# Last stage of a four-layer block: round two's opening and round one's closing moved beside other work

## Chip, cores and metric

One Trainium2 chip, one core. The metric is device time in microseconds (us) of one launch. The kernel before takes 3154.64 us, the median of three runs (3143.95 to 3157.51 us).

## What is computed

The program runs four residual layers over x of shape (4, 1024, 128): a state-space layer, a mixture of experts with top-2 routing, an attention with two softmaxes and their difference, and last a layer of soft experts. The change touches the last one alone, so it is the one shown (`_layernorm` around it and within it, `_gating` for both of its halves):

```python
n1 = _layernorm(x, ln1_w, ln1_b)                       # x is itself a layernorm of the residual
rw = _gating(n1, smha_sim, smha_gates, 2)              # normalize, 8 logits, top 2, softmax
q = einsum('btc,ech,bte->bth', n1, q_proj, rw)         # and k, v: 8 experts each
attn = softmax(mask(q @ k.T * scale)) @ v              # causal, t = 1024
hs = x + einsum('bth,ehc,bte->btc', attn, o_proj, rw)
n2 = _layernorm(hs, ln2_w, ln2_b)
rw2 = _gating(n2, moe_sim, moe_gates, 2)
inter = gelu(einsum('btc,eci->btei', n2, w1))
return hs + einsum('btei,eic,bte->btc', inter, w2, rw2)
```

The result is normalized once more and added to the residual x, and that is the output.

## The kernel before

The stage works on the four batches in two rounds, r = 0 and r = 1. In each, batches k = 0 and k = 1 of the round run side by side: everything is written once per k, with its own half of PSUM (four banks, B[0] to B[3]) and its own SBUF tiles. In a round, per k:

- **Opening**: statistics and normalization of x into hs (`stats`, `norms`: DVE L256, L260, L265; the square root is `rstd` on POOL, L248 and L250), the same again into n1, weight and bias (DVE L1318, L1323), squares of n1 (POOL L1469), transposes of n1 (PE L1591) copied to xT (ACT L1518), eight logits per row (PE L1603), and the gate: normalize, top 2, softmax (DVE L1330 to L1370, POOL L1472, ACT L1522). It ends in the weights rw.
- **Projections**, 16 steps q (two halves of 512 rows by 8 experts). POOL multiplies n1 by one expert's weight (L1486), PE transposes the result into B[3] (`scaled`, L1614), ACT takes its high half (L1537), DVE its low half (L1392), and PE makes the products (L645 to L647 for q and k, L1665 for v). PE transposes step q + 1 just ahead of the products of q. A multiply of q waits for the transpose of q - 2, since s_sc has two buffers.
- **Attention**, 8 rows of blocks i: scores (PE L1625), mask and maximum (DVE L1406, L1408), exponential (ACT L1552), transposes (PE L1685) and copies (ACT L1560), the product with v (PE L1695), its scaling (DVE L1398), the reciprocal (DVE L1414).
- **Output**: 16 more multiplies, transposes (PE L1709), copies and products (PE L1723).
- **Second opening** for n2, with the same helpers, then the **experts** (PE L1738 and L1751, ACT L1579, DVE L1438, POOL add L1495).
- **Closing**: statistics and normalization of hs into lnb, and the addition to X (POOL L1502); SP stores it.

What sets the order: each engine has one instruction queue, in order. For each engine there are two generators (`soft_dve(e, 0)`, `soft_dve(e, 1)` and so on), one per k, that yield planned times; `weave` always takes the generator with the smallest time. The planned times decide only the order of the instructions in a queue; the waits on semaphores decide when each runs. The plan is in `D_LN`, `D_TR`, `D_GATE`, `D_ATT`, `d_scaled`, `d_proj`; round two has the same plan `D_PERIOD = 193` later:

```python
def weave(*streams):
    ...
    while live:
        s = min(live)
        t = next(s[2], None)
```

Since a generator goes through a round and then through the next, all of round two of one k stands behind all of its round one in every queue.

Of the kernel before, what the change touches and what calls it, by code (L numbers as in the profile page):

```python
# [104 lines left out]
def program(nc, d, out):  # L105
    ctx = ExitStack()
    with ctx:
# [1085 lines left out]
        def d_at(k, r, t):  # L1193
            return D_PERIOD * r + D_SHIFT * k + t

        def d_scaled(k, r, q, more=0.0):

            if q >= 16:
                return d_at(k, r, D_OUT + D_STEP * (q - 16) - 1.5 + more)
            h, x = q // 8, q % 8  # L1200
            return d_at(k, r, 24 + 26.2 * h if x == 0 else 25 + 26.2 * h + D_EXPERT * (x - 1))

        def d_proj(k, r, q, more=0.0):
            return d_at(k, r, 25 + 26.2 * (q // 8) + D_EXPERT * (q % 8) + more)
# [4 lines left out]
        def two(name, *ordered):  # L1209

            return [Tick(sem(f"{name}{k}"), [(r, *x) for r in range(2) for x in ordered]) for k in range(2)]

        t_dtr = two("t_dtr", (0, 0), (0, 1), (0, "logits"), (2, 0), (2, 1), (2, "logits"))
# [5 lines left out]
        a_dtr = two("a_dtr", (0, 0), (0, 1), (0, "exp"), (2, 0), (2, 1), (2, "exp"))  # L1219
# [3 lines left out]
        v_dln = two("v_dln", *keys(4, ("stats", "out")))  # L1223
        v_dgt = two("v_dgt", *keys((0, 2), ("sumsq", "logits", "pre", "rw")))
# [3 lines left out]
        p_dln = two("p_dln", *[x for w in range(4) for x in [(w, "rstd")] + ([(2 * w - 2, "sq"), (2 * w - 2, "norm")]  # L1228
                                                                              if w in (1, 2) else [])])
# [10 lines left out]
        s_hs, s_n1, s_q, s_k, s_v = [[MA[:, 5120 * k + 1024 * i:5120 * k + 1024 * i + 1024] for k in range(2)]  # L1240
                                     for i in range(5)]
        s_hs, s_n1, s_v = [[x.rearrange("p (j c) -> p j c", c=128) for x in y] for y in (s_hs, s_n1, s_v)]
# [4 lines left out]
        s_g = [big[7][:, 512 * k:512 * k + 512].rearrange("p (j n) -> p j n", j=8) for k in range(2)]  # L1247
# [55 lines left out]

        def soft_dve(e, k):
            s, L = st[f"d{k}"], s_L[k]
            hs, n1 = s_hs[k], s_n1[k]
            hst, n1t = [hs[:, j, :] for j in range(8)], [n1[:, j, :] for j in range(8)]
            B, S0, S1 = bank[4 * k:4 * k + 4], ps[2 * k], ps[2 * k + 1]

            def G(i):  # L1310
                return s_g[k][:, :, 8 * i:8 * i + 8]

            def affine(r, w):
                norms(e, s, hst, n1).then_inc(*dve_own.up())
                ready = dve_own.now()
                yield d_at(k, r, D_LN[w][1] + 1)
                e.wait_ge(*ready)
                e.tensor_tensor(n1, n1, lnp[:, 2 * w - 2:2 * w - 1, :].to_broadcast([128, 8, 128]), ALU.mult).then_inc(  # L1318
                    *dve_own.up())
                ready = dve_own.now()  # L1320
                yield d_at(k, r, D_LN[w][1] + 2)
                e.wait_ge(*ready)
                e.tensor_tensor(n1, n1, lnp[:, 2 * w - 1:2 * w, :].to_broadcast([128, 8, 128]), ALU.add).then_inc(  # L1323
                    *v_dln[k].up(r, w, "out"))

            def gating(r, w, times):
                which = w // 2
                yield d_at(k, r, times[1])
# [548 lines left out]
```

## Time and profile before

| what | value |
|---|---|
| median of three runs | 3154.64 us (3143.95 to 3157.51) |
| the profiled execution, its own time | 3154.66 us |
| its span, first to last instruction | 3152.5 us |
| mean granted TensorE clock | 0.869 |
| busy: PE, DVE, ACT, POOL | 2425.7, 2198.9, 1710.0, 1415.3 us |
| the last stage | from 2505.4 us to the end |
| round one of it: projections | 2553.7 to 2636.2 us |
| round one: attention, output | 2636.2 to 2689.1, 2689.1 to 2731.9 us |
| round one: experts on PE | 2751.8 to 2818.0 us |
| round two: first transpose of the projections | 2869.6 us |

The page gives busy times by engine over the whole span, the span in 40 slices, the chain that ended last and the costliest groups. Busy shares over the whole program say little here, since four layers with different limits stand one behind the other; the stage is read from the timeline and from tables of stretches. The granted clock is 1.00 at full speed (2.4 GHz) and 0.50 at half of it (1.2 GHz).

### The profile page before, as it was taken

What the parts mean: (1) busy time and instruction counts of PE and PEld (TensorE: products, weight loads), DVE (VectorE), ACT (ScalarE), POOL (GpSimd) and SP (SyncE); (2) the same over time, 40 slices, a digit from 0 to 9 for tenths busy, and PEclk for the clock granted to TensorE, in tenths of its full rate; (3) what the DMA queues carried; (4) which work ended last, traced back from release to release, by engine and by line L of the source; (5) the groups of instructions that cost most, each with busy time, mean ns of one, the idle gap of its engine ahead of it and who ended that gap; (6) DMA issues with size and microseconds to landing.
All of it is one profiled execution on the core that took longest, in us unless ns stands there. A gap on an engine that the chain in (4) does not pass through costs nothing.

```text
span 3152.5 us, 42236 instructions
## 1 busy us (share of the span) xinstructions
PE 2425.7 (77%) x15570; PEld 1750.1 (56%) x15570; DVE 2198.9 (70%) x3701; ACT 1710.0 (54%) x2608; POOL 1415.3 (45%) x1331
## 2 busy tenths in 40 slices
PE   3114776677667687799999999999999569876987
PEld 1002455344345565477777777777777456755675
DVE  3995698699699612588878887887888543355334
ACT  4223664666376242588777877787778323222332
POOL 0341144144224300365765676657656641564156
PEclk8556888788788888799999999999999879887988
DMA  3000000000000000100000010010000100000000
GB/s 100 0 0 0 0 1 1 1 1 1 1 1 1 1 1 14 41 21 21 21 21 21 21 28 21 20 26 21 21 24 9 41 1 1 1 14 1 1 1 14
DMA packets 32029, 42.02 MB, mean 13 GB/s; under 512 B 8897, under 2 KB 18130, under 8 KB 31442
## 3 DMA queue, kind: packets, MB, share of 16 engines
q1 hardware_dynamic: 31826, 39.34, 4.6%
q8 instruction: 125, 2.05, 0.3%
q14 instruction: 78, 0.64, 0.1%
HBM read 12.05 MB, written 2.10 MB: 4 GB/s over the span
## 4 chain that ended last, share of the span: by engine, by line
PE 46%; issue 19%; DVE 17%; POOL 12%; ACT 4%; SPq 1%; DMA 0%; POOLq 0%; ACTq 0%; DVEq 0%
PE ps L954 10%; PE ps L932 6%; PE ps L943 6%; POOL MA L379 5%; DVE MA L1090 3%; PE ps L710 3%; PE ps L914 2%; PE ps L1723 2%; DVE lnb L265 2%; PE ps L645 2%; PE ps L647 1%; PE ps L646 1%; PE ps L1665 1%; POOL MA L1173 1%; PE ps L1625 1%
## 5 line engine op out<-in xcount | busy, mean ns | idle before, releaser
L1090 DVE TENSOR_REDUCE MA<-ps 128x1 f32<-128x1024 f32 x512 | 623.3, 1221 | 195.3 <-PE ps L932 182.7
L379 POOL TENSOR_TENSOR MA<-MA,BIG 128x1024 f32<-128x1024 f32 x120 | 280.2, 2356 | 624.9 <-DVE BIG L350 624.9
L954 PE MATMUL ps<-MA,WB 128*64 128x128 f32 x4096 | 502.5, 276 | 0.0
L954 PEld LDWEIGHTS ps<-MA,WB 128*64 128x64 f32 x4096 | 440.7, 137 | 88.4 <-issue 87.4
L344 DVE TENSOR_TENSOR_SCAN BIG<-BIG 128x1024 f32<-128x1024 f32 x128 | 347.1, 2751 | 0.0
L932 PE MATMUL ps<-BIG 96*128 96x512 f16 x1024 | 314.6, 389 | 13.5 <-ACT WB L1017 5.1
L632 ACT ACTIVATE HR<-ps,b 128x512 f32<-128x512 f32 x288 | 191.6, 687 | 243.9 <-PE ps L647 242.9
L710 PEld LDWEIGHTS ps<-WB,HR 128*128 128x128 f32 x2304 | 307.3, 210 | 24.9 <-issue 8.6
L710 PE MATMUL ps<-WB,HR 128*128 128x128 f32 x2304 | 314.4, 295 | 0.0
L1017 ACT ACTIVATE WB<-ps,MA 128x1024 f32<-128x1024 f32 x206 | 229.6, 1115 | 149.8 <-DVE MA L1090 149.8
L497 PE MATMUL ps<-bc,sel 96*128 96x512 bf16 x256 | 108.3, 520 | 247.1 <-DVE BIG L350 190.8
L1024 ACT ACTIVATE MA<-ps 128x1024 f32<-128x1024 f32 x256 | 259.9, 1015 | 6.0 <-PE ps L943 6.0
L1486 POOL TENSOR_TENSOR BIG<-MA,BIG 128x512 f32<-128x512 f32 x128 | 132.1, 1049 | 232.3 <-PE ps L1709 74.5
L436 ACT ACTIVATE BIG<-MA,aneg 128x1024 f32<-128x1024 f32 x128 | 141.5, 1142 | 109.9 <-DVE BIG L344 105.8
L1017 ACT ACTIVATE MA<-ps,MA 128x1024 f32<-128x1024 f32 x153 | 170.7, 1116 | 45.7 <-DVE MA L1090 45.6
L1147 POOL TENSOR_TENSOR MA<-MA 128x2 f32<-128x2 f32 x128 | 25.2, 197 | 369.5 <-DVE MA L1094 369.5
L497 PEld LDWEIGHTS ps<-bc,sel 96*128 96x128 bf16 x256 | 22.3, 113 | 300.1 <-DVE BIG L350 213.1
L943 PE MATMUL ps<-ident,WB 128*128 128x128 f32 x1232 | 165.9, 278 | 5.9 <-POOL WB L1159 3.1
L943 PEld LDWEIGHTS ps<-ident,WB 128*128 128x128 f32 x1232 | 144.4, 144 | 45.1 <-DVE WB L1099 10.6
L645 PE MATMUL ps<-xT,WB 128*128 128x512 f16 x288 | 126.4, 439 | 52.9 <-ACT HR L632 48.7
L589 DVE SCALAR_TENSOR_TENSOR acc<-ps,g,acc 128x128 f32<-128x128 f32 x256 | 71.1, 338 | 123.1 <-PE ps L710 123.1
L340 DVE TENSOR_TENSOR BIG<-MA,ps 128x1024 f32<-128x1024 f32 x128 | 149.8, 1210 | 1.2 <-PE ps L497 1.2
(290 smaller groups left out, 5166.3 us busy)
## 6 DMA issues: line engine op xcount, KB each, us to landing
BIG<-BIG SPq DMA_DIRECT2D x192, 64.0 KB, 2.0
BIG<-WB SPq DMA_DIRECT2D x192, 64.0 KB, 2.0
WB<-w_dram SPq DMA_DIRECT2D x1, 2304.0 KB, 14.7
X<-x_dram SPq DMA_DIRECT2D x4, 512.0 KB, 12.6
HR<-w_dram SPq DMA_DIRECT2D x1, 2048.0 KB, 9.4
out_dram<-X SPq DMA_DIRECT2D x4, 512.0 KB, 3.2
WB<-wqkv_dram SPq DMA_DIRECT2D x1, 1536.0 KB, 6.7
WB<-w_dram SPq DMA_DIRECT2D x2, 512.0 KB, 9.1
```

The costliest lines, as they stand in the source:

```text
L340: e.tensor_tensor(db[k][c], du[:, c, :], ps[0][:, :], ALU.mult).then_inc(*v_mtb.up(b, n, c))
L344: e.tensor_tensor_scan(db[k][c], da[k][c], db[k][c], 0.0, ALU.mult, ALU.add).then_inc(*v_mscan.up(b, n, c))
L379: e.tensor_tensor(yy[:, c, :], yy[:, c, :], db[n % 2][c], ALU.add).then_inc(*p_my.up(b, n, c))
L632: e.activation(hr[(4 * k + f) % 8], bank[4 + f % 2], ACT.Gelu, bias=small["b1"][:, PLAN[k][1], f:f + 1], scale=BACK).then_inc(*a_fg.up(b, ...
L645: e.matmul(o, w[0], x[0], start=first, stop=False)
L710: i = e.matmul(o, hr[(4 * kk + f) % 8][:, 128 * j:128 * j + 128], w2[:, x, f, :], start=f == 0 and x != 8, stop=f == 3)
L932: x = e.matmul(ps[s][:, 512 * h:512 * h + 512], stack[q % 2][0:96, 0, 2 * pp + s, 128 * i:128 * i + 128], stack[q % 2][0:96, 1, 2 * pp + s ...
L943: x = e.transpose(ps[2][:, 128 * k:128 * k + 128], P_of(n, 0)[:, 128 * k:128 * k + 128], ident[:, :])
L954: x = e.matmul(bank[6][64 * pp:64 * pp + 64, 0:128], V[(4 * b + g) % 2][:, k, 64 * pp:64 * pp + 64], DT[n % 2][:, 128 * k:128 * k + 128], ...
L1017: e.activation(P_of(n, s), ps[s][:, :], ACT.Exp, bias=L[:, 2 * s + pp:2 * s + pp + 1], scale=1.0, accum_out=L[:, 4 + 2 * s + pp:5 + 2 * s ...
L1024: e.activation(DT[n % 2], ps[2][:, :], ACT.Copy, scale=1.0).then_inc(*a_at.up(n))
L1090: e.tensor_reduce(L_of(n)[:, c:c + 1], ps[s][:, :], AX, ALU.max, negate=True).then_inc(*v_amx.up(n, s))
```

## The change

Round two's opening gets generators of its own (`front_pe`, `front_act`, `front_dve`, `front_pool`, one for each r and k), and so does each round's closing (`last_dve`, `last_pool`). With their own planned times (`F_LN`, `F_TR`, `F_LOGITS`, `F_GATE`, `D_LN[1]`) their instructions stand among those of the other generators: round two's normalizations among round one's projections (planned 32 to 55), its transposes and logits between the projections and the scores (75.2, 77.6), its gate in round one's attention (78.2 to 88); round one's closing (191.5 and 195.5) among round two's projections, since `D_PERIOD` goes from 193 to 164. Buffers: hs, n1 and the gate's tile exist once per round (n1 of round two in what was `sel`, its gate tile in `acc`), the experts' products go to `s_tmp` instead of `s_sc`. Round two's transposes and logits use bank B[3] for both halves, so the second transpose waits for ACT's copy of the first, and the first product with v waits until DVE has read the logits. In the gate, the part from the subtraction on has a planned time of its own behind both k's first part. No arithmetic is added or left out.

```diff
-        D_PERIOD, D_EXPERT, D_SHIFT = 193.0, 3.15, 0.0
-        D_LN = [(0, 3), (5, 8), (139.5, 142.5), (187.5, 190.5)]
-        D_TR = [11, 110, 145.5]
-        D_GATE = [(13, 16, 19, 22), (145.5, 148.5, 151.5, 154.5)]
+        D_PERIOD, D_EXPERT = 164.0, 3.15
+        D_LN, D_TR, D_LOGITS, D_GATE = [(139.5, 142.5), (191.5, 195.5)], 145.5, 151.5, (145.5, 148.5, 151.5, 152, 154.5)
+        F_LN = [[(0, 3), (5, 8)], [(32, 36), (40, 44)]]
+        F_TR, F_LOGITS, F_GATE = [11, 75.2], [18.9, 77.6], [(13, 16, 19, 19.5, 22), (49, 55, 78.2, 82, 88)]
...
+        def front_dve(e, k, r):
+            s, hs = st[f"d{k}"], s_hs[k][r]
+            xs, hst = [tile_of(k + 2 * r, j) for j in range(8)], [hs[:, j, :] for j in range(8)]
+            yield F_LN[r][0][0]
+            stats(e, s, xs, {}).then_inc(*v_dln[k].up(r, 0, "stats"))
+            yield F_LN[r][0][1]
+            e.wait_ge(*p_dln[k].at(r, 0, "rstd"))
+            norms(e, s, xs, hs).then_inc(*v_dln[k].up(r, 0, "out"))
+            yield F_LN[r][1][0]
+            stats(e, s, hst, {0: v_dln[k].at(r, 0, "out")}).then_inc(*v_dln[k].up(r, 1, "stats"))
+            yield F_LN[r][1][1]
+            e.wait_ge(*p_dln[k].at(r, 1, "rstd"))
+            yield from d_affine(e, k, r, 1, F_LN[r][1])
+            yield from d_gate(e, k, r, 0, F_GATE[r], bank[4 * k + (3 if r else 2)])
...
+        def last_dve(e, k, r):
+            s, hst = st[f"d{k}"], [s_hs[k][r][:, j, :] for j in range(8)]
+            yield d_at(r, D_LN[1][0])
+            stats(e, s, hst, {0: p_dm[k].at(r, 15)}).then_inc(*v_dln[k].up(r, 3, "stats"))
+            yield d_at(r, D_LN[1][1])
+            e.wait_ge(*p_dln[k].at(r, 3, "rstd"))
+            if r:
+                e.wait_ge(*p_dx[k].at(r - 1))
+            norms(e, s, hst, lnb[k]).then_inc(*v_dln[k].up(r, 3, "out"))
...
+        def front_pool(e, k, r):
+            for w in range(2):
+                yield F_LN[r][w][0]
+                d_root(e, k, r, w)
+            yield from d_norm(e, k, r, 0, F_GATE[r])
...
+                for q in range(32):
+                    h, x = q // 8 % 2, q % 8
+                    yield d_scaled(r, q, -4 if r and q < 2 else 0)
...
+                    if q >= 2:
+                        e.wait_ge(*t_dst[k].at(r, q - 2))
+                    elif r:
+                        e.wait_ge(*t_dst[k].at(r - 1, 30 + q))
...
+        def last_pool(e, k, r):
+            yield d_at(r, D_LN[1][0])
+            d_root(e, k, r, 3)
+            yield d_at(r, D_LN[1][1])
+            e.wait_ge(*v_dln[k].at(r, 3, "out"))
...
+        def front_act(e, k, r):
+            B = bank[4 * k:4 * k + 4]
+            yield F_TR[r]
+            d_turned(e, k, r, 0, (B[3], B[3]) if r else B)
+            yield F_GATE[r][3] + 2
+            d_exp(e, k, r, 0)
...
+        def d_turn(e, k, r, w, banks):
+            for h in range(2):
+                e.wait_ge(*v_dln[k].at(r, max(w, 1), "out"))
+                if w == 0 and r:
+                    if h:
+                        e.wait_ge(*a_dtr[k].at(1, 0, 0))
...
+        def front_pe(e, k, r):
+            B = bank[4 * k:4 * k + 4]
+            yield F_TR[r]
+            d_turn(e, k, r, 0, (B[3], B[3]) if r else B)
+            yield F_LOGITS[r]
+            d_logits(e, k, r, 0, B[3 if r else 2])
...
                     else:
                         e.wait_ge(*v_dlo[k].at(r, 15))
+                        if r == 0:
+                            e.wait_ge(*v_dgt[k].at(1, 0, "logits"))
```

How the queues change, at three places. **POOL, round one's projections.** Before, all 64 multiplies of the projections and of the output (L1486) stand in a row:

```order
L1472 TENSOR_TENSOR BIG<-BIG,half 128x8 x2
L1486 TENSOR_TENSOR BIG<-MA,BIG 128x512 x64
L248 TENSOR_SCALAR st_d<-st_d 128x8
```

Now (the multiply is L1502, the squares are L1477):

```order
L1502 TENSOR_TENSOR BIG<-MA,BIG 128x512 x8
L248 TENSOR_SCALAR st_d<-st_d 128x8
L250 TENSOR_TENSOR st_d<-st_d,half 128x8
L248 TENSOR_SCALAR st_d<-st_d 128x8
L250 TENSOR_TENSOR st_d<-st_d,half 128x8
L1502 TENSOR_TENSOR BIG<-MA,BIG 128x512 x4
L248 TENSOR_SCALAR st_d<-st_d 128x8
L250 TENSOR_TENSOR st_d<-st_d,half 128x8
L248 TENSOR_SCALAR st_d<-st_d 128x8
L250 TENSOR_TENSOR st_d<-st_d,half 128x8
L1502 TENSOR_TENSOR BIG<-MA,BIG 128x512 x4
L1477 TENSOR_TENSOR BIG<-sel 128x1024 x2
```

Two pairs of square roots and one pair of squares now stand between the multiplies of steps 3 and 4, 5 and 6, 7 and 8.

**POOL, from round one's experts to round two's projections.** Now (L1514 is the experts' addition, L1502 the multiply of round two, L1523 the addition to X):

```order
L1514 TENSOR_TENSOR MA<-MA,BIG 128x512 x31
L1502 TENSOR_TENSOR BIG<-sel,acc 128x512 x2
L1514 TENSOR_TENSOR MA<-MA,BIG 128x512
L1502 TENSOR_TENSOR BIG<-sel,acc 128x512 x2
L248 TENSOR_SCALAR st_d<-st_d 128x8
L250 TENSOR_TENSOR st_d<-st_d,half 128x8
L248 TENSOR_SCALAR st_d<-st_d 128x8
L250 TENSOR_TENSOR st_d<-st_d,half 128x8
L1502 TENSOR_TENSOR BIG<-sel,acc 128x512 x4
L1523 TENSOR_TENSOR X<-X,lnb 128x1024 x2
L1502 TENSOR_TENSOR BIG<-sel,acc 128x512 x56
```

The closing's roots stand behind the multiplies of steps 0 and 1, its additions to X behind those of steps 2 and 3.

**DVE, round one's attention**, row of blocks 1 to row 2. Before (L1414 reciprocal, L1406 mask, L1408 maximum):

```order
L1414 RECIPROCAL BIG<-BIG 128x1 x2
L1406 TENSOR_TENSOR ps<-ps,tri 128x128
L1408 TENSOR_REDUCE BIG<-ps 128x1
```

Now the first rows of what stands behind the reciprocals (L1431 is the reciprocal; L1349 to L538 are subtraction and top 2 of one k):

```order
L1431 RECIPROCAL BIG<-BIG 128x1 x2
L1349 TENSOR_TENSOR acc<-acc,sgm 128x8x8
L527 MAX acc<-acc 128x8 x8
L531 MAX_INDEX gi<-acc 128x8 x8
L534 CAST acc<-gi 128x8x8
L537 TENSOR_TENSOR acc<-iota,acc 128x8x8
L538 TENSOR_TENSOR acc<-iota,acc 128x8x8
L1349 TENSOR_TENSOR acc<-acc,sgm 128x8x8
```

All of the gate from the subtraction to the exponential, for both k, stands between the reciprocals of row 1 and the mask of row 2.

## Rows read from the trace of the kernel before

**Rows 1.** The page: the head.
```profile
span 3152.5 us, 42236 instructions
```
**Rows 2.** Busy times by stretch: stretch, its length, busy (instructions) of PE, PEld, DVE, ACT, POOL, PEclk, DMA.
```profile
2553.70:2636.20 82.50, 80.20 (x705) 56.19 (x705) 22.05 (x33) 23.61 (x41) 32.20 (x31) 0.96 0.00 1
2636.20:2689.10 52.90, 43.38 (x267) 32.34 (x265) 22.13 (x63) 25.57 (x60) 4.11 (x4) 1.00 0.00 1
2818.00:2869.60 51.60, 10.33 (x50) 10.23 (x49) 46.01 (x237) 4.19 (x7) 28.38 (x22) 0.54 0.07 21
```
**Rows 3.** Timeline, one step of the projections: start, length, instruction, [idle before, releaser].
```profile
2603.41 0.60 PE L1614 MATMUL ps<-ident,BIG 128*128 128x128 f32 x4
2608.21 0.60 PE L1614 MATMUL ps<-ident,BIG 128*128 128x128 f32 x4
...
2605.76 0.69 DVE L1392 SCALAR_TENSOR_TENSOR BIG<-ps,BIG 128x512 f16<-128x512 f32 x1 [0.39 <-ACT BIG L1537]
...
2604.09 2.13 POOL L1486 TENSOR_TENSOR BIG<-MA,BIG 128x512 f32<-128x512 f32 x2 [2.68 <-PE ps L1614]
```
**Rows 4.** Timeline from round one's last expert products to round two's first products.
```profile
2814.28 3.73 PE L1751 MATMUL ps<-WB,HR 128*128 128x128 f32 x32
...
2816.14 4.93 POOL L1495 TENSOR_TENSOR MA<-MA,BIG 128x512 f32<-128x512 f32 x4 [1.02 <-DVE BIG L1438]
...
2873.08 0.63 PE L645 MATMUL ps<-BIG,WB 128*128 128x512 f16 x1
```
**Rows 5.** Timeline, round two's first statistics and square roots.
```profile
2830.69 1.63 DVE L256 BATCH_NORM_STATS2 st_d<-X 128x6 f32<-128x128 f32 x8
...
2835.71 1.71 POOL L250 TENSOR_TENSOR st_d<-st_d,half 128x8 f32<-128x8 f32 x1
```
**Rows 6.** Timeline, round two's normalization into n1, weight, bias and squares.
```profile
2843.95 4.39 DVE L265 TENSOR_SCALAR MA<-MA,st_d 128x128 f32<-128x128 f32 x16
...
2851.83 4.66 POOL L1469 TENSOR_TENSOR BIG<-MA 128x1024 f32<-128x1024 f32 x2 [5.66 <-DVE MA L1323]
```
**Rows 7.** Timeline, round two's closing.
```profile
3139.62 6.43 DVE L265 TENSOR_SCALAR lnb<-MA,st_d 128x128 f32<-128x128 f32 x16
...
3141.84 2.34 POOL L1502 TENSOR_TENSOR X<-X,lnb 128x1024 f32<-128x1024 f32 x1
```
**Rows 8.** Timeline, the start of round one's attention.
```profile
2634.40 0.60 ACT L1542 ACTIVATE MA<-ps 128x512 f32<-128x512 f32 x1 [4.63 <-PE ps L647]
...
2636.19 0.44 PE L1625 MATMUL ps<-MA 128*128 128x128 f32 x2
2638.81 0.92 PE L1625 MATMUL ps<-MA 128*128 128x128 f32 x4 [2.18 <-ACT MA L1543]
...
2640.51 0.70 PE L1625 MATMUL ps<-MA 128*128 128x256 f32 x2 [0.66 <-ACT WB L1552]
...
2643.30 0.28 DVE L1406 TENSOR_TENSOR ps<-ps,tri 128x128 f32<-128x128 f32 x1
```
**Rows 9.** Logits of both k; then DVE's busy time in the gate's three parts.
```profile
2747.89 4.07 PE L1603 MATMUL ps<-simn,xT 128*128 128x8 f32 x32
...
2545.43:2548.10 2.67, 2.53 (x29) 0.50 0.00 0
2549.23:2551.53 2.30, 2.16 (x18) 0.50 0.00 0
```
**Rows 10.** PE busy and granted clock around three pauses of PE.
```profile
509.90:515.20 5.30, 0.01 (x1) 1.00 0.00 0
515.20:518.50 3.30, 3.26 (x8) 0.50 0.00 0
...
533.47:539.10 5.63, 5.29 (x23) 0.50 0.00 0
...
2744.78:2747.51 2.73, 2.73 (x13) 0.50 0.00 0
2747.51:2750.90 3.39, 3.39 (x33) 1.00 0.02 5
```

More of the change, by code:

```diff
@@ L1222, in program @@
         a_dg = two("a_dg", *keys(16))
-        v_dln = two("v_dln", *keys(4, ("stats", "out")))
-        v_dgt = two("v_dgt", *keys((0, 2), ("sumsq", "logits", "pre", "rw")))
+        v_dln = two("v_dln", *keys((2, 3), ("stats", "out")), front=keys(2, ("stats", "out")))
+        v_dgt = two("v_dgt", *keys((2,), ("sumsq", "logits", "pre", "rw")), front=keys((0,), ("sumsq", "logits", "pre", "rw")))
         v_dlo, v_dat = two("v_dlo", *keys(16)), two("v_dat", *[x for i in range(9) for x in
@@ L1302, in experts_pe, with d_affine @@
             e.matmul(bank[0][:, 0:16], ones[:, :], lsq[:, 0:16], start=True, stop=True).then_inc(*t_dsp.up(0))
+        def d_affine(e, k, r, w, times):
+            s, hs, n1 = st[f"d{k}"], s_hs[k][r], s_n1[k][r]
+            norms(e, s, [hs[:, j, :] for j in range(8)], n1).then_inc(*dve_own.up())
+            ready = dve_own.now()
+            yield times[1] + 1
+            e.wait_ge(*ready)
+            e.tensor_tensor(n1, n1, lnp[:, 2 * w - 2:2 * w - 1, :].to_broadcast([128, 8, 128]), ALU.mult).then_inc(
+                *dve_own.up())
+            ready = dve_own.now()
+            yield times[1] + 2
+            e.wait_ge(*ready)
+            e.tensor_tensor(n1, n1, lnp[:, 2 * w - 1:2 * w, :].to_broadcast([128, 8, 128]), ALU.add).then_inc(
+                *v_dln[k].up(r, w, "out"))
@@ L1304, in soft_dve @@
         def soft_dve(e, k):
             s, L = st[f"d{k}"], s_L[k]
-            hs, n1 = s_hs[k], s_n1[k]
-            hst, n1t = [hs[:, j, :] for j in range(8)], [n1[:, j, :] for j in range(8)]
-            B, S0, S1 = bank[4 * k:4 * k + 4], ps[2 * k], ps[2 * k + 1]
+            B, S0 = bank[4 * k:4 * k + 4], ps[2 * k]
             def G(i):
[L1311 to L1324, printed above, removed]
@@ new lines, in d_turn @@
+        def d_turn(e, k, r, w, banks):
+            for h in range(2):
+                e.wait_ge(*v_dln[k].at(r, max(w, 1), "out"))
+                if w == 0 and r:
+                    if h:
+                        e.wait_ge(*a_dtr[k].at(1, 0, 0))
+                    else:
+                        e.wait_ge(*v_dlo[k].at(0, 15))
+                for j in range(4):
+                    i = e.transpose(banks[h][:, 128 * j:128 * j + 128], s_n1[k][r][:, 4 * h + j, :], ident[:, :])
+                i.then_inc(*t_dtr[k].up(r, w, h))
@@ new lines, in d_logits @@
+        def d_logits(e, k, r, w, o):
+            e.wait_ge(*a_dtr[k].at(r, w, 1))
+            if w:
+                e.wait_ge(*v_dom[k].at(r, 1))
+            elif r == 0:
+                e.wait_ge(*v_dsp.at("simn"))
+            for j in range(8):
+                i = e.matmul(o[:, 8 * j:8 * j + 8], xT[k][:, 128 * j:128 * j + 128], simn[:, w // 2, :], start=True, stop=True)
+            i.then_inc(*t_dtr[k].up(r, w, "logits"))
+        def front_pe(e, k, r):
[4 more added lines that the diff above has]
+            d_logits(e, k, r, 0, B[3 if r else 2])
@@ L1784, in _ @@
             e.wait_ge(phase, 8)
-            weave(experts_pe(e), soft_pe(e, 0), soft_pe(e, 1))
+            weave(experts_pe(e), *[front_pe(e, k, r) for r in range(2) for k in range(2)],
+                  soft_pe(e, 0), soft_pe(e, 1))
         @block.scalar
@@ L1794, in _ @@
             e.wait_ge(phase, 8)
[L1795 removed]
+            weave(experts_act(e), *[front_act(e, k, r) for r in range(2) for k in range(2)],
+                  soft_act(e, 0), soft_act(e, 1))
         @block.vector
```

370 lines of the change are left out of this document (161 added, 209 removed).

## The prediction

> **What bounds the kernel now.** I read the page first: the span is 3152.5 us [rows 1], and the profiled execution's own time is 3154.66, 2.2 more. That is 0.02 over the median of the runs shown, so the sum below stands against 3154.66. The page's shares mix four layers, so the stage is read from the table of stretches [rows 2] and then from the timeline. In round one's projections PE is the bound: 80.2 of 82.5 us busy, POOL 32.2, DVE 22.1. In its attention the engines wait for each other: PE 43.4 of 52.9, DVE 22.1. Between the rounds lie 51.6 us in which DVE is busy for 46.0 and PE for 10.3, at a clock of 0.54: closing and opening, one small instruction after another. This gap is what the change can win.
>
> **What goes: the gap.** PE ends round one's last expert product at 2818.01, and round two's first product starts at 2873.08 [rows 4]. Now POOL's queue decides. Its last four additions start at 2816.14 and take 1.23 each. Three of them, then k = 0's two multiplies (1.07 each, [rows 3]), the fourth addition and k = 1's first multiply end at 2824.3. Two groups of transposes at half clock (some 0.9 each, twice what they take of a step at full clock) bring the first product to 2826.1. Gain: 47.0 us. Bounds: 44 (a slip of POOL) and 50 (clock still full).
>
> **What comes: the opening beside the projections.** The DVE time itself is covered: a step lasts 4.80 us (two transposes of k = 0, 2603.41 and 2608.21), DVE ends its second low half 3.04 us after the first transpose [rows 3] and is idle for 3 us, and a low half that is late by up to 3 us is not missed. The queue of POOL is not covered. PE transposes step q + 1 before the products of q, so it stands still until POOL's multiply of q + 1 is done, and that multiply now stands behind a square root that waits for DVE's statistics, which stand behind the low half of step q.
> - Step 3 to 4: low half +3.04, statistics and both roots 6.73 (2830.69 to 2837.42, [rows 5]), multiply 1.07: 10.84 instead of 4.80, a stall of 6.0.
> - Step 5 to 6: the same chain, with DVE 0.4 late from the normalizations before (4.39, [rows 6]): 6.4.
> - Step 7 to 8: from the start of the normalizations to the end of the squares 12.54 [rows 6]; 3.04 + 12.54 + 1.07 = 16.65. Without the change the transpose comes 8.7 later (a step, and one without its transposes, an estimate of 3.9). Stall 7.9.
>
> Sum 20.3, bounds 14 and 24. No multiply can run ahead, since there are two buffers.
>
> **The opening beside the attention.** Before, ACT copies q and k from 2634.40 on, under the last products of v, and the scores start at 2636.19 [rows 8]. Now ACT's copies of round two's transposes stand ahead. They alternate with PE through one bank: transposes, copy, transposes, two copies, transposes, copy, seven times some 0.6 and the handovers, 4.4. Then q and k of k = 0, 1.1: the scores start 5.5 later. The second k's scores follow 2.62 behind as before, then 4.07 us of logits on PE [rows 9]; so row 1's scores start 12.4 after 2636.19 instead of 4.3: 8.1. Behind it DVE does 2.67 + 2.67 + 2.30 us of gate [rows 9] in front of the mask of row 2, which DVE reached at 2643.30 without a pause [rows 8]: 7.6. The gate's end (bounds 0 and 2.3) I take at 1. Sum 16.7, bounds 9 and 20.
>
> **The closing beside round two's projections.** Its statistics and roots stand between the multiplies of steps 1 and 2: the stall of 6.0 again, less 0.9 since that step runs at half clock and covers more: 5.1. The additions to X stand before step 4. One more row counts here: in the tail, the second k's normalization is ready when the first addition (2.34) starts, takes 4.2 us beside it instead of 2.2, and the pair lasts 6.43 [rows 7]. So: 3.04, normalization 2.2, the second one 4.2, the second addition 2.34, multiply 1.07: 12.85 against 4.80, stall 8.0. Without that contention it would be 6.1. The Trainium skill, page SBUF — State Buffer, section "SBUF: two separate sides", calls the port pair of DVE and GpSimd "an exclusive lock, not a bandwidth split"; by it the 8.0 stands, and rows 7 agree. Sum 13.1, bounds 9 and 15.
>
> **The clock.** Rows 10 show PE pausing for 5.3 us from full clock and going on at half clock for 3.30; in two more cases it runs at half for 5.63 and 2.73 before it is back. Half of that is lost: some 2.0 a pause. The five stalls above are each as long as that first pause: 10. The pause behind the gate costs 2, and if the logits run at half clock they cost up to 2.8 more; I take 1. Sum 13. Bounds: 0, and 22.
>
> **Small.** In round one's own opening k = 0's top 2 now waits for k = 1's logits: 1.1. A table load ahead of round two's first exponential, mostly covered: 0.3. Together 1.4. The end of the program is as before. DMA is not touched: the two stores of round one go out beside other work, as their wait is SP's alone.
>
> **Sum:** -47.0 + 20.3 + 16.7 + 13.1 + 13 + 1.4 = +17.5 us, so 3172 us, slower by 0.55%. That is about what a measurement of this kernel can tell from no change (0.5%, 15.8 us: 3138.9 to 3170.4). The case's own range is 3160 to 3184, from the middle of the bounds.
>
> **Rivals.**
> - *The clock stays full* (same). The stalls are there, but PE's activity on both sides keeps the clock up. Then 13 falls away: -47.0 + 51.5 = +4.5, 3159 us. Against it: the pause of 5.3 us in rows 10. For it: the 82.5 us of projections hold 0.96 although PE has idle moments. Chance 0.14.
> - *POOL's queue is not the stall* (faster). If the roots come earlier than I have it (statistics that DVE slips into its idle 3 us one step ahead), PE stays the bound in both projections, and the stalls of 33.4 and their clock of 10 go. Left are the attention, 3 for its clock and 1.4: -47.0 + 21.1 = -26, 3129 us. It decides from the point where the five stalls come to under 16 us. Against it: the order printed above, in which nothing can slip. Chance 0.15.
> - *Half clock through the attention* (much slower). Round one's attention begins with 8 us in which PE does little but transposes and logits, then pauses behind the gate. If the clock stays down for half of the attention, PE's 43.4 busy us [rows 2] become half as many again, of which some 20 lie on the path: 3192 us. The Trainium skill, page TensorE: Matmul & The Clock Gate, section "Part 4: PE-mode transpose", says that transposes do not count as busy for the clock; by it this case would come true. But from 2744.78 PE does transposes alone, at half clock, and goes on at full from 2747.51 [rows 10]: the trace speaks against the rule. Chance 0.13.
> - The stated case: 0.58.
>
> **How the numbers follow.** Of the stated case some seven in ten lie over 3170.4 (0.38) and three in ten under (0.19); with the third rival slower is 0.50; with the first same is 0.33; faster, the second rival and a rest, is 0.17. The range takes in the stated case, the first rival and most of the third, and reaches down toward the second: 3134 to 3192.
>
> **What would show it.** In the trace after: PE idle for 6 to 8 us three times in round one's projections, in front of a transpose, released by POOL's multiply, and POOL in front of it waiting for DVE's aggregate; twice the same in round two's projections, the second with a normalization of over 4 us beside an addition to X; round one's projections 103 us and more instead of 82.5; scores 5.5 us behind the last product of v, 4 us of logits, and DVE busy for 7.6 us between row 1 and row 2; half clock behind each pause; and about 8 us instead of 55 between the last expert product and the first product of round two. I am wrong if the projections keep to some 85 us (second rival), if the clock in them stays 1.00 (first), or if the attention takes over 90 us (third).

## The result and the profile after

The changed kernel takes 3179.02 us (median of four runs, 3175.12 to 3179.57) against 3154.32 us of the kernel before on the same chip (four runs): ratio 1.0081, 95% interval 1.0057 to 1.0106. It is slower. A second set of four runs gave 3179.31 us, ratio 1.0076 (1.0051 to 1.0100). The profiled execution took 3178.65 us, 24.0 more than that of before. The forecast was 3172 us, or 17.5 more. This program also has a slower state at a lower granted clock; in this document only two runs fell into it, 3291.57 and 3290.99 us of experiment 7 (clock 0.77 instead of 0.87), and no comparison uses them.

The head of the page of the changed kernel, which answers to [rows 1]:

```profile
span 3176.8 us, 42234 instructions
```

Busy times by stretch of the changed kernel (stretch, its length, busy and instructions of PE, PEld, DVE, ACT, POOL, then PEclk and DMA): round one's projections, its attention, last expert product to first product of round two, and round two from there to its scores. The first three answer to [rows 2]:

```profile
2551.36:2664.97 113.61, 90.64 (x720) 61.71 (x720) 45.95 (x135) 25.53 (x45) 47.16 (x44) 0.86 0.00 1
2664.97:2735.27 70.30, 55.48 (x296) 42.74 (x297) 31.94 (x149) 26.54 (x62) 4.11 (x4) 0.85 0.00 1
2864.45:2872.38 7.93, 2.46 (x14) 2.10 (x13) 1.38 (x2) 1.12 (x2) 7.20 (x7) 0.77 0.01 2
2872.38:2970.58 98.20, 83.50 (x693) 56.51 (x692) 31.91 (x79) 22.41 (x40) 37.53 (x34) 0.90 0.04 12
```

The gap is gone: 7.93 us stand where 55.07 stood, from 2818.01 to 2873.08 in [rows 4]. But the stretches that took in its work grew by more. Stretch by stretch, in us, with the forecast worked out from the terms of the sum:

| stretch | before | after | difference | forecast |
|---|---|---|---|---|
| before the stage | 2505.4 | 2502.3 | -3.0 | 0 |
| round one's opening | 48.3 | 49.1 | +0.8 | +1.1 |
| projections, to the first score | 82.5 | 113.6 | +31.1 | 20.3 + 5.5 + 6 of clock = 31.8 |
| attention | 52.9 | 70.3 | +17.4 | 11.2 + 3 of clock = 14.2 |
| last expert product to round two's first product | 55.1 | 7.9 | -47.2 | -47.0 |
| round two, first product to scores | 79.8 | 98.2 | +18.4 | 13.1 + 4 of clock = 17.1 |
| round two's attention | 53.9 | 57.2 | +3.3 | 0.3 |
| its output and second opening, then the experts | 126.5 | 129.8 | +3.3 | 0 |
| round one's output and experts, and the tail | 148.1 | 148.5 | +0.4 | 0 |

The projections are PE-bound no longer: PE is busy for 90.6 of 113.6 us. The chain of work that ended last shows why. Two parts of it, between steps 3 and 4 and between steps 7 and 8 (start, length, what):

```profile
2568.07 0.69 DVE BIG L1409
2568.76 1.56 DVE st_d L256 x8
...
2573.62 1.67 POOL st_d L250
2575.29 1.02 POOL BIG L1502
2576.35 1.12 PE ps L1641 x4
...
2604.06 0.69 DVE BIG L1409
2604.75 4.10 DVE sel L265 x16
...
2612.33 4.66 POOL BIG L1477 x2
2616.99 1.01 POOL BIG L1502
2618.05 1.13 PE ps L1641 x4
```

Read from the bottom of each part: PE's transpose waits for POOL's multiply (L1502). The multiply stands behind a square root (L250) or behind the squares (L1477). Those wait for DVE's statistics or normalizations, which DVE begins only after its low half (L1409) of the step. No engine is short of capacity there. The first pause as PE has it, from its timeline (start, length, instruction, [idle before, releaser]); the others there, ahead of 2594.65 and of 2618.05, are 5.67 and 7.45 us long, with the same releaser:

```profile
2576.35 1.12 PE L1641 MATMUL ps<-ident,BIG 128*128 128x128 f32 x4 [5.67 <-POOL BIG L1502]
```

Forecast were 6.0, 6.4 and 7.9. The clock behind them, busy times by stretch: the first pause and what follows it; last, the start of the attention:

```profile
2570.68:2576.35 5.67, 0.00 (x1) 0.00 (x0) 2.48 (x21) 0.00 (x0) 4.91 (x6) 0.90 0.00 1
2576.35:2582.10 5.75, 5.75 (x18) 3.23 (x19) 2.52 (x7) 1.19 (x2) 2.97 (x3) 0.50 0.01 3
...
2667.40:2681.10 13.70, 13.41 (x50) 11.50 (x51) 5.35 (x35) 3.14 (x11) 0.00 (x0) 0.50 0.00 1
```

Behind the pause PE works without a break for 5.75 us at half clock. In the attention 13.7 us run at half clock, and the logits stand in them. From the timeline of the changed kernel, PE and DVE at the attention's start:

```profile
2665.01 0.49 PE L1652 MATMUL ps<-MA 128*128 128x128 f32 x2 [1.66 <-ACT MA L1564]
...
2668.27 6.83 PE L1621 MATMUL ps<-simn,xT 128*128 128x8 f32 x32
...
2674.96 1.20 PE L1652 MATMUL ps<-MA 128*128 128x256 f32 x2
...
2679.63 0.21 DVE L1349 TENSOR_TENSOR acc<-acc,sgm 128x64 f32<-128x64 f32 x1
...
2688.87 2.08 PE L1652 MATMUL ps<-MA 128*128 128x512 f32 x2 [6.06 <-ACT WB L1573]
```

The logits take 6.83 us, not the 4.07 of [rows 9], and row 1's scores start 9.95 us after the first instead of the 4.3 of [rows 8]. From 2679.63 DVE works on the gate while row 2 waits; PE's pause there is 6.06 us. What PE did ahead of the fall to half clock is sparse work: it was busy for 2.24 of the 5.50 us from 2659.50 on (round two's transposes) and for 0.49 of the next 2.4 us.

In the closing, DVE, POOL and PE from the timeline of the changed kernel:

```profile
2894.28 6.28 DVE L265 TENSOR_SCALAR lnb<-MA,st_d 128x128 f32<-128x128 f32 x16
...
2896.49 2.44 POOL L1523 TENSOR_TENSOR X<-X,lnb 128x1024 f32<-128x1024 f32 x1 [9.77 <-DVE lnb L265]
...
2883.75 1.12 PE L1641 MATMUL ps<-ident,BIG 128*128 128x128 f32 x4 [5.20 <-POOL BIG L1502]
...
2904.03 1.12 PE L1641 MATMUL ps<-ident,BIG 128*128 128x128 f32 x4 [7.75 <-POOL BIG L1502]
```

Both pauses are there, 5.20 and 7.75 us (forecast: 5.1 and 8.0). The same normalizations alone, split where the first addition starts:

```profile
2894.28:2896.46 2.18, 2.18 (x9) 1.00 0.00 0
2896.46:2900.56 4.10, 4.09 (x8) 0.87 0.15 45
```

The first k's take 2.18 us, the second's beside the addition 4.10, as in [rows 7]. The lengths of the single ones, shortest, median and longest in ns, show how:

```profile
L265 DVE TENSOR_SCALAR lnb<-MA,st_d x16: 332/341/2436, 2894.3 to 2900.2; 128x128 f32<-128x128 f32 x16
```

One of the sixteen stands for 2.44 us, as long as POOL's addition beside it; the others go on at their usual pace.

So each mechanism of the forecast is seen. The open questions: whether the queue's order alone makes the pauses, or DVE's added work; what the half clock costs; and whether the gap can be had without the price.

### The profile page after: what moved, and what is told of

Same layout as the page of the kernel before. It is cut to its first block, busy times and chain, and to the rows that moved or that the text cites. A ratio compares the mean times of both kernels' runs of the same rounds, so it can differ in the third digit from the quotient of the medians.

```text
span 3176.8 us, 42234 instructions
## 1 busy us (share of the span) xinstructions
PE 2440.9 (77%) x15570; PEld 1756.9 (55%) x15570; DVE 2197.2 (69%) x3701; ACT 1709.5 (54%) x2608; POOL 1412.1 (44%) x1331
## 4 chain that ended last, share of the span: by engine, by line
PE 46%; issue 19%; DVE 17%; POOL 13%; ACT 4%; SPq 1%; DMA 0%; POOLq 0%; ACTq 0%; DVEq 0%
PE ps L954 10%; PE ps L932 6%; PE ps L943 6%; POOL MA L379 5%; DVE MA L1090 3%; PE ps L710 3%; PE ps L914 2%; PE ps L1752 2%; DVE lnb L265 2%; PE ps L645 2%; PE ps L647 1%; PE ps L646 1%; PE ps L1652 1%; PE ps L1641 1%; POOL MA L1173 1%
## 5 line engine op out<-in xcount | busy, mean ns | idle before, releaser
L1017 ACT ACTIVATE sel<-ps,MA 128x1024 f32<-128x1024 f32 x102 | 113.8, 1116 | 49.0 <-DVE MA L1090 49.0
```

The costliest lines, as they stand in the source:

```text
L1017: e.activation(P_of(n, s), ps[s][:, :], ACT.Exp, bias=L[:, 2 * s + pp:2 * s + pp + 1], scale=1.0, accum_out=L[:, 4 + 2 * s + pp:5 + 2 * s ...
```

## The experiments

All stand against the kernel before on the same chip (medians 3152.46 and 3153.42 us in two sets of runs, 3153.04 in the third). The names of the parts are those of the table. The changed kernel was measured in other sets of runs than most of these, so "less than the changed kernel" compares medians of different sets, in which the kernel before differs by up to 1.9 us; the lengths of the stretches don't depend on that. No arithmetic is changed except where it is said.

**1. The opening's square roots and squares later in POOL's queue.** Nothing moves on DVE, PE or ACT.

```diff
+        F_ROOT, F_SQ = [(0, 5), (38, 44.2)], [13, 52]
...
-                yield F_LN[r][w][0]
+                yield F_ROOT[r][w]
                 d_root(e, k, r, w)
-            yield from d_norm(e, k, r, 0, F_GATE[r])
+            yield from d_norm(e, k, r, 0, (F_SQ[r],) + F_GATE[r][1:])
```

> The changed kernel, but on POOL round two's opening stands later: the square roots behind the multiplies of steps 5 and 7 (instead of 3 and 5), the squares behind that of step 9 (instead of 7). DVE's order is untouched, so all its statistics and normalizations stay in front of the same low halves. Theory (POOL's queue makes PE's pauses): the pauses of 5.7, 5.7 and 7.5 us in round one's projections go, but for 1 to 2 us at the half, and the half clock behind them; the projections take 92 to 95 us instead of 113.6, the kernel 3179 - 20 = 3159 us. Rival (DVE's 4.5 and 9 us blocks in front of the low halves make them): the pauses stay, projections 113, kernel 3179.

Measured: 3162.46 us, ratio 1.0028 (1.0018 to 1.0038), 16.6 less than the changed kernel. Busy times of the projections, then one row of POOL's timeline:

```profile
2548.97:2643.69 94.72, 84.27 (x720) 58.78 (x720) 49.72 (x135) 25.35 (x45) 47.28 (x43) 0.95 0.00 1
```

```profile
2568.00 0.25 POOL L248 TENSOR_SCALAR st_d<-st_d 128x8 f32<-128x8 f32 x1 [2.54 <-DVE st_d L260]
```

The projections fall from 113.6 to 94.7 us and their clock rises from 0.86 to 0.95; the attention stays, at 70.7. DVE does the same work beside them. POOL now waits 2.54 us in front of the first root (12.46 in the changed kernel), since two multiplies run first. The queue made these pauses. One of 4.3 us stays, in the middle of the projections, where I had expected 1 to 2, and its chain is another: DVE's weight and bias, then the low half, then PE:

```profile
2593.54 2.27 DVE sel L1319 x2
...
2598.08 0.61 DVE BIG L1410
...
2598.83 1.07 PE ps L1642 x4
```

So with the queue mended DVE is next, at one place, for 4.3 us.

**2. Round one's closing later in POOL's queue.** Planned times of the roots and of the additions to X:

```diff
         def last_pool(e, k, r):
-            yield d_at(r, D_LN[1][0])
+            yield d_at(r, 196)
             d_root(e, k, r, 3)
-            yield d_at(r, D_LN[1][1])
+            yield d_at(r, 202)
```

> The changed kernel, but on POOL the closing's roots stand behind the multiply of step 3 (instead of 1) and its additions to X behind that of step 5 (instead of 3). Theory: the pauses of 5.2 and 7.8 us in round two's projections go and the half clock behind them; they take 80 to 84 us from first product to first score instead of 98.2, the kernel 3179 - 15 = 3164 us. Rival (DVE's blocks): no difference, 3179.

Measured: 3153.33 us, ratio 1.0004 (0.9995 to 1.0014), no different from before. Round two, first product to scores, and its attention, busy times by stretch:

```profile
2868.36:2948.38 80.02, 77.76 (x693) 53.91 (x692) 31.82 (x79) 22.41 (x39) 36.60 (x34) 0.98 0.05 14
2948.38:3002.58 54.20, 44.52 (x268) 33.34 (x265) 22.23 (x63) 26.87 (x61) 4.11 (x4) 0.97 0.00 1
```

80.0 us is what the stretch took before (79.8), so the closing is now free. The time is 10.7 us under what I had expected, and 25.7 under the changed kernel. In the profiled executions 18.2 of it lie in the stretch itself, 3.0 in the attention behind it, 1.3 in what follows that, and the rest in parts ahead of the edit, where two executions differ by some 4 us anyway. The expectation had priced the pauses and too little of the clock behind them, above all nothing in the attention.

**3. The gate in round one's output instead of its attention.** DVE's subtraction to exponential and what follows it are planned at 112 and 122:

```diff
-        ... F_GATE = ... (49, 55, 78.2, 82, 88)]
+        ... F_GATE = ... (49, 55, 78.2, 112, 122)]
...
-            yield F_GATE[r][3] + 2
+            yield F_GATE[r][3] + (6 if r else 2)
```

> The changed kernel, but the gate of round two from its subtraction on stands in round one's output stage (planned 112 to 122 instead of 82 to 88), where DVE was busy for 2.4 of 42.8 us in the kernel before. Theory: the pause of 6.1 us in the attention goes with its half clock, nothing new waits; from first score to first output transpose 60 to 62 us instead of 70.3, the kernel 3179 - 9 = 3170 us. Rival (the attention is long because its start is at half clock, and DVE is covered): 3177 to 3181.

Measured: 3169.49 us, ratio 1.0055 (1.0038 to 1.0071). The stretch from scores to output:

```profile
2661.47:2724.32 62.85, 54.14 (x296) 42.69 (x297) 23.35 (x69) 26.01 (x60) 4.11 (x4) 0.86 0.00 1
```

7.4 us less (70.3 before the edit, 60 to 62 expected), PE's pause of 6.06 is gone, and the stretch behind it, from the output to the experts, takes 63.2 us against 62.7. The gate block costs what it held the mask up for, and 10.0 us over the 52.9 of [rows 2] stay: they belong to logits and transposes.

**4. The three edits together.**

> The three moves together. Theory: the gains add, since they lie in different stretches: -20, -15 and -9, the kernel at 3179 - 44 = 3135 us, 20 us under the kernel before. Rival (PE's bound or clock gives part of it back): 3145 to 3160.

Measured: 3131.89 us, ratio 0.9932 (0.9916 to 0.9949). The projections take 94.7 us as in experiment 1, round two's products to scores 80.0 as in experiment 2. The attention:

```profile
2645.09:2705.84 60.75, 51.86 (x296) 40.61 (x297) 23.25 (x69) 25.89 (x60) 4.11 (x4) 0.89 0.00 1
```

Alone the edits gave 16.6, 25.7 and 9.5 us, 51.8 in sum; together 47.1. The parts are nearly independent. The idea of the change pays when the moved instructions stand where their inputs are ready.

**5. The clock alone: PE kept busy in the pauses.** In the changed kernel, matmuls whose result is overwritten unread stand in front of the transposes that wait. They multiply constants; the outputs are not touched by them.

```diff
             def scaled(r, q):
+                fill = {(0, 4): 11, (0, 6): 11, (0, 8): 15, (1, 2): 10, (1, 4): 15}.get((r, q), 0) if k == 0 else 0
+                if fill:
+                    e.wait_ge(*v_dlo[k].at(r, q - 1))
+                    for _ in range(fill):
+                        e.matmul(B[3], ident[:, :], lnp[:, :, :].rearrange("p a c -> p (a c)"), start=True, stop=True)
                 e.wait_ge(*p_dsc[k].at(r, q))
```

> The changed kernel with extra matmuls on PE, all of them thrown away (each writes bank B[3] just before a transpose overwrites it): 11, 11 and 15 in the three pauses of round one's projections, 10 and 15 in the two of round two's, 0.43 us each at full clock, so that each group ends inside its pause. They keep PE busy and change no wait. Theory (half clock behind each pause costs some 2 us a pause): the clock stays 1.00 in both projections, they take 113.6 - 6 = 107 to 109 and 98.2 - 4 = 93 to 95 us, the kernel 3179 - 10 = 3169 us. Rival (the clock behind the pauses costs nothing, as other engines are waited for): 3179, or more.

Measured: 3186.55 us, ratio 1.0112 (1.0091 to 1.0134): slower, not faster. PE's timeline in the first pause:

```profile
2569.53 9.66 PE L1639 MATMUL ps<-lnp,ident 128*128 128x512 f32 x22
```

Each f32 matmul stands there as two instructions of 0.44 us, so eleven take 9.66 us in a pause of 5.67. The experiment was built wrong: it lengthened the pauses and said nothing of the clock's price. Again, with half as many (6, 6, 8 in round one; 5, 8 in round two):

> The changed kernel with 6, 6 and 8 (round one) and 5 and 8 (round two) discarded f32 matmuls of 128x512 in front of the transposes that wait for POOL's multiply: half as many as in the run before, whose matmuls took 0.88 us each, not 0.43, and outlasted the pauses by 3.8, 3.8 and 5.3. Now 5.3, 5.3 and 7.0 us of them against pauses of 5.67, 5.67 and 7.45. Theory (the clock costs what its half-clock stretches show behind each pause): the clock stays at 1.00 in the projections, round one's take 106 to 108 us instead of 113.6, round two's products to scores 92 to 95 instead of 98.2; time about 3167. Rival (the steps behind a pause are set by the low half and POOL's buffers, so the clock is covered): within 1.5 us of 113.6 and 98.2, time 3177 to 3180.

Measured: 3167.70 us, ratio 1.0048 (1.0031 to 1.0064), 11.3 less than the changed kernel (9.0 by the profiled executions, in which the projections start 2.5 us later than in its own). Projections, and round two's products to scores; then the first pause and what follows it:

```profile
2553.95:2660.86 106.91, 100.47 (x760) 65.10 (x761) 45.69 (x135) 25.57 (x45) 47.10 (x43) 0.97 0.00 1
2869.89:2962.59 92.70, 89.55 (x720) 58.73 (x718) 31.92 (x79) 22.41 (x39) 37.51 (x34) 0.98 0.04 13
```

```profile
2572.49:2578.32 5.83, 5.37 (x15) 2.15 (x13) 2.64 (x24) 0.00 (x0) 4.91 (x6) 1.00 0.00 1
2578.32:2585.20 6.88, 6.88 (x58) 4.91 (x59) 5.17 (x18) 2.08 (x4) 2.97 (x3) 1.00 0.01 2
```

The wait is as long as before (5.83 us with the fillers in it), but the clock is 1.00 in it and behind it. The projections save 6.7 us and round two's stretch 5.5: 12.2 us for five pauses, 2.4 each. Both lie in the range I had given. Round two's attention takes 54.1 us here instead of 57.2. Not all of this is kept. Round one's attention takes 71.3 us instead of 70.3, and round two from its output to the last expert product 131.9 instead of 129.8, since there the logits run at half clock again (6.84 us, as in the kernel before).

**6. Only the additions to X later.** The closing's roots stay where the change put them:

```diff
             d_root(e, k, r, 3)
-            yield d_at(r, D_LN[1][1])
+            yield d_at(r, 202)
             e.wait_ge(*v_dln[k].at(r, 3, "out"))
```

> The changed kernel with one edit: round one's two additions to X stand two steps later in POOL's queue (behind the multiplies of steps 4 and 5 of round two); the square roots stay where they are. Theory (the second closing pause is POOL waiting for normalizations that a running addition to X slows): the two normalization groups take 4.4 to 4.6 us instead of 6.28, the pause of 7.75 in front of step 4's transposes falls under 2.5, the pause of 5.20 stays, products to scores 86 to 90 instead of 98.2; time about 3168. Rival 1 (POOL's multiply slows the normalizations just as well): 6 us and over for the pair, but the pause gone all the same. Rival 2 (DVE's normalizations themselves hold the low half and so PE): a pause of 4 or more stays, products to scores 93 or more.

Measured: 3167.63 us, ratio 1.0045 (1.0029 to 1.0062). Round two's products to scores, and rows of the timeline:

```profile
2872.64:2960.47 87.83, 80.65 (x694) 55.22 (x692) 31.75 (x79) 22.41 (x39) 37.42 (x34) 0.94 0.05 13
```

```profile
2894.45 6.30 DVE L265 TENSOR_SCALAR lnb<-MA,st_d 128x128 f32<-128x128 f32 x16
...
2896.66 2.46 POOL L1523 TENSOR_TENSOR X<-X,lnb 128x1024 f32<-128x1024 f32 x1 [2.36 <-DVE lnb L265]
```

98.2 falls to 87.8 us. The pause of 7.75 is gone and that of 5.20 stays (5.21). My number for the normalizations was wrong: I expected 4.4 to 4.6 us, and they take 6.30, since the addition still starts beside the second k's. POOL had done the two multiplies by 2894.30 and got to the addition as early as before. So the slow normalization goes on and costs PE almost nothing (0.23 us of idle time at the next transposes). It had a price only while a multiply stood behind the addition that waited for it. What the slowing by itself adds to the pause, 1.9 us by its rows, was not measured apart.

**7. The affine part of round two's normalization split off**, on top of experiment 4: weight and bias one step later than the normalization itself.

```diff
-        F_LN = [[(0, 3), (5, 8)], [(32, 36), (40, 44)]]
+        F_LN = [[(0, 3), (5, 8)], [(32, 36), (40, 44, 51.5, 55)]]
...
-        F_ROOT, F_SQ = [(0, 5), (38, 44.2)], [13, 52]
+        F_ROOT, F_SQ = [(0, 5), (38, 44.2)], [13, 58]
```

> The kernel with all three moves (3132 us), and round two's multiplication by weight and addition of bias on DVE no longer in one block of 9 us in front of step 8's low half, but behind step 9's and step 10's, squares and their sum later still. Theory: the last pause in round one's projections, 4.3 us where the kernel before had 1.9, goes back to 1.9 and its half clock goes; projections 90.5 to 92 instead of 94.7 us, kernel 3128 us. Rival (the pause is of PE's own and ACT's copies at the half): 3132.

Two runs took 3126.23 (the profiled one) and 3130.19 us. The projections take 91.9 us instead of 94.7, with no pause of 4.3. The kernel once more:

> The same kernel as the one with the affine part of the normalization split off, run again because two of its four times lay at 3291 and two at 3126 and 3130. If the 3291 belongs to the kernel (a second mode of it), it comes up again in about half of the runs; if it was a disturbance of those minutes, all runs lie at 3124 to 3132. From the segments: 3128.

Measured: 3127.76 us (3126.30 to 3129.55), ratio 0.9921 (0.9905 to 0.9938). No time near 3291 came back in four runs, and nothing here rests on it. Against experiment 4 this is 4.1 us less, of which the projections give 2.9; the rest is within what two sets of runs differ by.

**8. Round two's transposes and logits in the pause ahead of round one's second opening**, its gate beside the experts, on top of experiment 7:

```diff
-        F_TR, F_LOGITS, F_GATE = [11, 75.2], [18.9, 77.6], [(13, 16, 19, 19.5, 22), (49, 61, 78.2, 112, 122)]
+        F_TR, F_LOGITS, F_GATE = [11, 138], [18.9, 139], [(13, 16, 19, 19.5, 22), (49, 61, 158, 164.3, 171)]
```

The signals and waits that go with the gate and the transposes are put in the new order, and POOL's part of the gate is planned at 78.2, round one's attention. In all kernels up to here PE stands idle for 12.93 us in front of the second opening's transposes.

> As e7, and round two's transposes and logits no longer stand between round one's projections and scores, but in the pause of 12.9 us on PE ahead of round one's second opening; the gate from the logits on beside round one's experts. Theory: the start of the attention is as in the kernel before, so from first transpose to first output transpose 135 to 139 us (82.5 + 52.9 = 135.4 in the kernel before, 155 in the one with three moves); the gate beside the experts costs two table loads and a pause or two, 2 to 5 us; kernel 3128 - 12 = 3116 us, and at most 3120. Rival (PE's work at the scores was hidden by the attention's own waits): 3128 or more.

Measured: 3115.71 us, ratio 0.9881 (0.9858 to 0.9903). Projections, attention, output with second opening:

```profile
2550.98:2636.48 85.50, 80.50 (x704) 56.19 (x705) 49.80 (x135) 23.59 (x41) 47.15 (x43) 0.97 0.00 1
2636.48:2689.41 52.93, 43.42 (x267) 32.38 (x265) 22.13 (x63) 25.56 (x60) 4.11 (x4) 1.00 0.00 1
2689.41:2755.23 65.82, 60.15 (x483) 59.64 (x481) 19.65 (x64) 21.92 (x40) 40.41 (x36) 0.86 0.00 1
```

The attention is back at 52.9 us with a clock of 1.00, and the place of the former gap takes 7.88 us. Against the kernel before, the work of the change still costs 3.0 us in the projections and 3.1 in front of the experts. This is the fastest kernel of the study: 38 us under the one before, 63 under the changed one.

## Why the prediction was right

**The gap** (forecast -47.0): -47.2. The additions on POOL, then the multiplies, then transposes at half clock, as worked out from [rows 3] and [rows 4].

**POOL's queue** (20.3 in round one, 13.1 in round two): the pauses measure 5.67, 5.67 and 7.45 against 6.0, 6.4 and 7.9, and 5.20 and 7.75 against 5.1 and 8.0. That is 31.7 us against 33.4, with the same releaser at each. Experiments 1, 2 and 6 take them away by POOL's order alone, with DVE's order and work unchanged, all but the 4.3 us behind DVE, so the rival in which the queue is not the stall falls. The durations came from rows of before that stood 250 us away from where they were used, and held.

**The opening beside the attention** (16.7): the start is right in kind. From PE's first transpose of round two's n1, 2659.44, to the first scores, 2665.01, are 5.57 us, where 5.5 were forecast; as much is left of the projections' +31.1 when the pauses (18.8) and the clock (6.7) are taken off. The gate in front of row 2's mask was to cost 7.6, 1 for its end and 2 of clock; experiment 3 gives 7.4 for all of it. **Here one term was mis-sized**: the logits' clock, and with it that of the rows behind them. I had put it at 1 of up to 2.8. The logits ran wholly at half clock, 6.83 instead of 4.07 us, and the half clock went on through rows 1 and 2. Logits and transposes cost 10.0 us in the attention (experiment 3) where my terms gave 3.6. The two errors partly cancel, which is luck, and leave 3.2 us: 17.4 for 14.2.

**The clock** (13): measured for the five long pauses as 12.2, where their part was 10. The rival in which the clock stays full falls, and so does that of half clock through the attention: its clock is 0.85, not half, and it takes 70.3 us, not 90. The Trainium skill, page TensorE: Matmul & The Clock Gate, section "Part 4: PE-mode transpose", says that a transpose doesn't count as PE-busy in the same way. The attention's start can't decide it: ahead of the 13.7 us at half clock PE did transposes, but with idle time for ACT's copies between them. The rows of before, from 2744.78 on, speak against it [rows 10]: the clock rose to full after 2.73 us of nothing but transposes.

**What the sum left out: 6.3 us behind the edits, of two causes.** Round two's attention is not touched by the change and was forecast at +0.3. It took 3.3 more, and so did the rest up to the last expert product. The rows, of before and then of the changed kernel: attention, and experts.

```profile
2952.88:3006.78 53.90, 44.87 (x267) 33.24 (x265) 22.14 (x63) 25.56 (x60) 4.11 (x4) 0.97 0.00 1
3072.60:3133.29 60.69, 59.54 (x321) 41.80 (x321) 28.18 (x85) 20.60 (x35) 36.83 (x30) 0.95 0.00 1
```

```profile
2970.65:3027.81 57.16, 47.49 (x267) 35.78 (x265) 22.23 (x63) 26.87 (x61) 4.11 (x4) 0.91 0.00 1
3090.58:3157.61 67.03, 61.06 (x322) 43.43 (x321) 30.84 (x114) 20.61 (x35) 37.59 (x31) 0.92 0.00 1
```

*The attention: the clock.* The attention has the same instructions on PE, DVE and POOL in both, PE is busy for 2.6 us more, and the clock is 0.91 instead of 0.97. In experiment 2 and in the second kernel of experiment 5, where both pauses of round two's projections are gone or filled, the attention takes 54.2 and 54.1. So 3.0 of the 3.3 us are the clock's. How the pauses bring this about is open. In the last 8 us ahead of the attention the clock is 1.00 in all these kernels. It falls only in the attention's own first 12 us, in which PE waits for ACT's copies: to a mean of 0.86 in the kernel before and in those two, to 0.72 in the changed kernel. And in experiment 6, with the pause of 7.75 us gone and that of 5.2 left, the attention still takes 57.2 us, at 0.72.

*The experts: the order of the gate.* In the changed kernel PE starts the experts earlier against the gate (its logits ran at full clock, 3.79 instead of 6.84 us, which gave 3.05 us back) and then waits 5.97 us for it instead of 1.15, and goes on at half clock; net +3.3. The clock ahead of them does not explain this. In the second kernel of experiment 5 attention, output and opening take what they took before (54.1, then 65.8 us, logits again 6.84), and the experts still take 5.4 us more:

```profile
3082.55:3148.67 66.12, 62.49 (x321) 43.95 (x321) 30.44 (x112) 20.58 (x35) 36.80 (x30) 0.90 0.00 1
```

Rows of before, then of that kernel:

```profile
3080.41 2.05 PE L1751 MATMUL ps<-WB,HR 128*128 128x128 f32 x16 [1.15 <-ACT HR L1579]
```

```profile
3082.80 0.23 DVE L1343 TENSOR_TENSOR BIG<-ps,BIG 128x64 f32<-128x64 f32 x1 [2.08 <-PE ps L1621]
...
3092.89 3.78 PE L1785 MATMUL ps<-WB,HR 128*128 128x128 f32 x16 [3.62 <-ACT HR L1600]
```

Before, DVE does k = 0's top 2 while PE is still at k = 1's logits. With the change it stands behind k = 1's first part, so DVE waits 2.08 us for those logits, the gate ends some 2.5 us later against the experts' start, and PE waits 3.62 us and goes on at half clock. The change gives the gates of all openings this order; the prediction priced it for round one's first opening (1.1) and put it at nothing in the second ones. In round one PE had waited 4.03 us for the gate before its experts already, and output, opening and experts together take only 0.4 us more. This cause is read from rows: no experiment puts the old order back.

**The sum.** 24.0 us measured against 17.5. The terms that missed: round one's attention +3.2, round two's attention +3.0 (clock), round two's experts +3.3 (order of the gate), round two's stretch +1.3, the other stretches +0.2 together, less 0.7 in the projections and 0.3 in the first opening; then -3.0 ahead of the stage, where the change does nothing and executions of one kernel differ by as much. They sum to 7.0, as the table does (24.5 against 17.5); by the spans the difference is 24.3 and by the executions' own times 24.0, the rest is rounding. The side, the place of each loss that was forecast and its releaser were as forecast. That the total comes as near as 6.5 us is in part luck: within the stage the profiled executions differ by 27.3 us, 9.8 over the forecast.

## What to carry to other kernels

When work is moved beside other work, go through every in-order queue that its small instructions enter. Square roots of 0.25 and 1.67 us held PE up for 5.7, since they stood in front of multiplies that were ready while their own input was not; two steps later they hold PE up no more. Look at every place where a shared helper is used: the gate's new order was priced in one opening and cost its time in another. Place each moved instruction by when its input is there, not by when its engine is free, and put PE's moved part into a pause that PE has anyway. For each pause of PE that a change makes, add what the half clock behind it costs (2.4 us here for pauses of 5 to 8 us), and look at the granted clock of stretches that the change doesn't touch: one of them took 3 us more by it here.

## What the runs showed of the hardware

- **Half clock behind a pause.** With PE idle for 5.67 us the next 5.75 us of work ran at half clock. With discarded matmuls in the same pause it ran at full. Filling the five pauses gave 11.3 us of the kernel's time; removing them gave 16.6 (round one's three) and 25.7 (round two's two). An f32 matmul of 128x512 stands in the trace as two instructions of 0.44 us, 0.88 in all at full clock.
- **Logits and the clock.** The logits are 32 instructions that keep PE at work without a gap, yet the clock does not rise in them: 6.83 us at half clock in the changed kernel. In [rows 10] the last transposes and then the logits (from 2747.89) run at full from 2747.51 to 2750.90, PE busy throughout, and the clock falls to half right then. The stretch behind it, of the kernel before:

```profile
2750.90:2757.70 6.80, 6.80 (x13) 3.42 (x13) 6.12 (x61) 0.00 (x0) 1.77 (x2) 0.50 0.00 1
```

  The 3.0 us ahead of the fall are logits alone, with no pause. PE's last pause ended at 2744.78, 6.1 us before the fall; whether it has a part in it, no run here shows. In these rows the logits neither raised the clock nor kept it for the stage behind them.
- **Normalization beside an addition.** DVE's normalizations of one k take 2.18 us alone and 4.10 beside POOL's addition to X; the pair takes 6.28, 6.30, 6.41 and 6.58 us in the changed kernel and in experiments 6, 4 and 2. The Trainium skill, page SBUF — State Buffer, section "SBUF: two separate sides", says of the port pair that DVE and GpSimd share that who starts first gets it for a whole instruction while the other blocks; on DVE's side it names instructions in a 2-port mode or with two SBUF inputs. The rows agree with a block of one whole instruction: a single normalization stands for 2.44 us beside the addition of 2.44 us, where the others take 0.34. POOL's addition is hardly touched: 2.44 us against 2.34 of the next one, which has no DVE instruction beside it. In which mode the normalizations run, no row shows.
